# Second attention of a routed-experts kernel: four pieces of ScalarE's hand-written order placed in other half steps

## The reference, cut to what matters

```
xn  = layernorm(x, g_in)
q   = (xn @ Wq)  -> 16 heads of 64, scaled;   k, v = xn @ Wkv  (one k and v for all heads)
sim = q k^T + bias, with a null key in front, causal and padding masks
z   = layernorm(softmax(sim) v @ Wo, g_out)
scores = sigmoid(z @ router_w.T);  the best 4 of 8 groups, in them the best 8 of 64 experts
x   = x + sum over the 8 experts e of w_e * relu2(z @ up_e) @ down_e + shared expert
```

## Time and profile before

| | |
|---|---|
| median of three runs | 1869.3 us (1865.94 to 1871.79) |
| the profiled execution's own time | 1868.09 us |
| its span, first to last instruction | 1866.2 us |
| mean granted TensorE clock | 0.938 |
| busy over the span | TensorE 83%, its weight loads 65%, VectorE 64%, GpSimd 50%, ScalarE 44% |
| second attention, half steps 0 to 63 | about 690 to 1242 us of the span |
| the 19 rounds behind them | to about 1350 us |
| second expert layer | about 1356 us to the end |

### The profile page before, as it was taken

One profiled execution on the slowest core, in us unless ns is written; L12 is line 12 of the kernel. 1 busy time (PEld: TensorE's weight loads), 2 busy tenths in 40 slices (PEclk: granted clock), 3 DMA queues, 4 the chain that ended last, 5 costly groups with the idle time before them and its releaser, 6 DMA issues. The chain is left out here.

```text
span 1866.2 us, 35427 instructions
## 1 busy us (share of the span) xinstructions
PE 1542.3 (83%) x12186; PEld 1216.8 (65%) x12187; DVE 1187.6 (64%) x2849; ACT 826.3 (44%) x1614; POOL 940.9 (50%) x840
## 2 busy tenths in 40 slices
PE   5699999987888869999999999975058888888880
PEld 2588888864655547776777776654058877776770
DVE  2677677745777655578878778787024455666674
ACT  2233333323545334565565555643036564555550
POOL 1233333335665521115555555567627767776672
PEclk9899999989999989999999999997579999999995
DMA  5278458011000000001111111136666678998875
GB/s 152 61 192 219 117 152 235 1 32 51 25 13 24 12 24 1 1 2 52 61 58 55 61 61 58 55 117 244 181 210 189 191 221 265 285 278 259 268 210 158
DMA packets 151371, 226.33 MB, mean 121 GB/s; under 512 B 24779, under 2 KB 123730, under 8 KB 149079
## 3 DMA queue, kind: packets, MB, share of 16 engines
q1 hardware_dynamic: 109062, 115.11, 22.1%
q0 software_dynamic: 27648, 67.44, 10.2%
q10 hardware_dynamic: 14544, 42.21, 7.0%
HBM read 110.31 MB, written 122.75 MB: 125 GB/s over the span
## 5 line engine op out<-in xcount | busy, mean ns | idle before, releaser
L1927 POOL DMA_INDIRECT y_rows<-se_ys,se_yidx x320 | 325.2, 1016 | 162.8 <-issue 95.8
L1100 POOL DMA_INDIRECT x_slots<-wide,a_sidx x256 | 257.2, 1005 | 72.5 <-issue 72.5
L443 POOL TENSOR_TENSOR e_hl<-e_h,e_hh 128x512 fp32r<-128x512 f32 x80 | 103.5, 1294 | 227.7 <-ACT e_hh L427 227.7
L1089 POOL TENSOR_TENSOR flat<-flat,a_rs 128x512 f32<-128x512 f32 x64 | 69.8, 1091 | 269.7 <-DVE a_rs L1581 269.7
L1970 PE MATMUL ps<-wide,se_hT 128*128 x640 | 157.8, 390 | 31.2 <-DVE se_ys L2060 30.9
L1947 PE MATMUL ps<-ident,se_xs 128*128 128x128 f32 x640 | 89.1, 285 | 100.8 <-DMA se_xs<-x_slots 83.2
L1958 PE MATMUL ps<-se_xsT,se_up 128*128 128x128 f32 x1280 | 166.1, 285 | 5.3 <-DVE se_hT L2049 4.3
L1958 PEld LDWEIGHTS ps<-se_xsT,se_up 128*128 128x128 f32 x1280 | 155.8, 199 | 13.6 <-issue 9.9
L1947 PEld LDWEIGHTS ps<-ident,se_xs 128*128 128x128 f32 x640 | 74.9, 146 | 121.4 <-issue 84.6
L1970 PEld LDWEIGHTS ps<-wide,se_hT 128*128 128x128 f32 x640 | 117.2, 193 | 50.6 <-issue 37.5
L1991 ACT COPY se_up<-w_up 128x256 f32 x320 | 105.8, 402 | 99.5 <-issue 78.6
(11 more groups left out here) (283 smaller groups left out, 3613.8 us busy)
## 6 DMA issues: line engine op xcount, KB each, us to landing
x_slots<-wide SPq DMA_DIRECT2D x40, 1032.0 KB, 14.3
se_xs<-x_slots SPq DMA_DIRECT2D x80, 516.0 KB
se_got<-y_rows ACTq DMA_DIRECT2D x64, 512.0 KB, 4.8
w_up<-in_up SPq DMA_DIRECT2D x8, 1024.0 KB, 18.1
y_rows<-se_ys,se_yidx POOLq DMA_INDIRECT x320
wide<-in_xT SPq DMA_DIRECT2D x2, 2048.0 KB, 10.2
flat<-in_x SPq DMA_DIRECT2D x8, 512.0 KB, 3.9
x_slots<-wide,a_sidx POOLq DMA_INDIRECT x256, 2.9
```

The lines of the kernel that those rows point to most:

```text
L1100: pool.indirect_dma_start(out=x_slots, out_offset=bass.IndirectOffsetOnAxis(ap=sidx[:, r % 2, t, k_:k_ + 1], axis=0), in_=stage[:, t, k_, ...
L1927: pool.indirect_dma_start(out=y_rows, out_offset=bass.IndirectOffsetOnAxis(ap=yidx[:, w % 2, b:b + 1], axis=0), in_=ys[:, w % 2, b, :], in ...
```

## The change

Only the order of ScalarE's program in the second attention is different. `normalized` for half 0 of the next block is called at the end of half step 7 of the block before it, where it was called in half step 0 (in block 0 it stays there too, for block 1). `normalized` for half 1 moves from half step 5 to half step 3. `stage_z` of tiles 0, 1 and 2 moves from ages 6, 8 and 10 to ages 7, 9 and 11; tile 3 stays at age 12. No instruction is added or taken away, and the orders of TensorE, VectorE, GpSimd and the DMA queues are the same.

```diff
                     elif age == 6:
                         square(r, 2)
                         square(r, 3)
-                        stage_z(r, 0)
-                    elif age in (8, 10, 12):
-                        stage_z(r, age // 2 - 3)
+                    elif age in (7, 9, 11, 12):
+                        stage_z(r, (7, 9, 11, 12).index(age))
...
                     if i == 0:
                         queries(b, 1, 2)
                         keys_values(b, 1)
-                        normalized(b + 1, 0)
+                        if b == 0:
+                            normalized(1, 0)
...
                     if i == 3:
                         queries(b + 1, 0, 1)
+                        normalized(b + 1, 1)
                     elif i == 5:
                         queries(b + 1, 0, 2)
                         queries(b + 1, 0, 3)
                         keys_values(b + 1, 0)
-                        normalized(b + 1, 1)
...
                     elif i == 7:
                         queries(b + 1, 1, 0)
                         queries(b + 1, 1, 1)
+                        normalized(b + 2, 0)
```

## The result

The changed kernel took 1856.6 us, the median of six runs (1850.09 to 1859.83), beside 1867.8 us for the kernel before in six runs on the same chip (1865.94 to 1871.79). The medians lie 11.2 us apart. The ratio on record, 0.9928 with a 95% interval of 0.9911 to 0.9945, is not the quotient of these two medians (0.9940) and says 13.4 us less, 10.3 to 16.6. The kernel is faster, by more than the 8.8 us of the forecast.

The account below looks back on a forecast made before the run. TensorE was taken to bound the stage, busy 69.6 of 74 us per block. Terms 6.0 + 2.8 + 0 = 8.8 us off the profiled 1868.1 gave 1859.3, plus 1.2 for the median: 1860.5 us, range 1854.5 to 1867.0.

Parts of the forecast that it names:

- Half step 2, 5 x 1.2 us: Blocks 2 to 6: TensorE's wait for VectorE's read shrinks from 1.47 to 0.3 us, 6.0 us won in all.
- Block 7's nearly unchanged wait: Block 7, half step 2: 1.36 us wait, put down to TensorE arriving an estimated 0.9 us earlier.
- Half step 6, 6 x 0.46 us: Blocks 1 to 6: without the normalizing ScalarE is in time for L1240, saving 0.46 us each, 2.8 us.
- The stagings: Half steps 1 and 3: the stagings of tiles 1 and 2, 2.0 us each, cost nothing.
- The reserve behind it: Behind half step 1's staging: ScalarE may be 1.3 us later before further lateness returns as TensorE's wait.
- Block 0, 0 us: Projection comes 1.85 us later in half step 4, 1.85 us sooner in half step 6; they cancel, 0 us.
- The clock, "I take neither": Block 0: 1.7 us of lower granted clock may vanish, or appear at half step 4; counted as nothing.
- Rival 1: Staging in half step 1 eats half step 2's gain if table switches hold ScalarE twice: 1866.5 us; chance 0.18.
- Rival 2: All of the 1.47 and 0.71 us waits goes, plus 1.7 us of clock in block 0: 1855.9 us; chance 0.14.
- Rival 3: Clock falls more often where TensorE stands still, two per block in seven blocks: slower, 1884 us; chance 0.04.
- Rival 4: ScalarE is late in half steps 3 and 4 by as much as early elsewhere: 1869.3 us; chance 0.06.

Follow-up runs that it names:

- block 0's edit: The whole change, but in block 0 the normalizing of half 1 is called in half step 4 instead of 3: 1855.8 us, ratio 0.9941.
- the run with two stagings: The change, but tiles 0 and 1 are both staged at age 9, in half step 1: a single run of 1863.0 us.

## Why the prediction was right and where it was wrong

**Half step 2, 5 x 1.2 us: right.** The wait went from 1.47 to 0.28 in blocks 2 to 6, 1.19 us each. The lateness was ScalarE's, handed on by VectorE. That either move alone cures it shows it twice more. Block 7's nearly unchanged wait is one of another kind, as argued: ScalarE was not late there (0.58 us idle before its copy), and from the transposes of half step 1 to its wait TensorE has 8.6 us of work, where it has 9.5 in block 2.

**Half step 6, 6 x 0.46 us: right,** 0.71 to 0.25 us in six blocks, and half 1's normalizing alone does it.

**The stagings: right that they cost nothing, but they also bring nothing.** The prediction counted both pieces, 3.9 us, against a lateness of 1.2, and did not say that one of them was enough. Their cover in half step 1 was used up exactly (0.30 us of reserve).

**The reserve behind it: right in size.** It was put at 0.3 + 1.0 = 1.3 us. ScalarE 1.7 us later made a block 0.39 us longer.

**Block 0, 0 us: right in the waits** (1.90 us instead of the 2.1 foretold at half step 4, none at half step 6). The prediction left out a third wait of before, 0.91 us of TensorE for the normalizing in half step 6 (L1181), but the sum still comes out near nothing: from half step 4 on, block 0 takes 28.1 us with the change, and 28.3 in the two executions of before that have no fall there.

**The clock, "I take neither": this is the step that failed.** The prediction put the clock at nothing. It looked for falls in block 0 alone, since the one block that it had read by stretches, block 3, stood at 1.00. Blocks 1, 4 and 5 of that same execution had falls, which the same view would have shown. Against that first profile the term is worth 4.0 us: 12.7 us of stage less 8.7 of waits. On the means of three executions it is about 2: 10.8 less 8.7. Of these 2.1 us, 1.1 lie in block 0 (0.6 of it is the fall of the earlier trace rows, worth 1.7 us and present in one execution of three, 0.2 are waits, and 0.3 the clock at the stage's start), 0.5 in blocks 2 to 6, 0.6 in block 7, and block 1 takes back 0.1.

How much of this the change caused is shown only in part. The falls in blocks 2 to 6 came with the wait of half step 2, the very one that the change removes: 12 in 25 blocks with it, none in 45 without it. Those in block 0 came with its wait in half step 6: 2 in 5 profiles with it, none in 9 without it. These two hold about 1.1 us. Block 1 keeps its stand, and behind it the clock fell in every profile of the change and in two of three of before; block 7 had a fall in every profile of the change and in one of three of before, where there were two; what these blocks gave or took is not explained.

**The sum.** The forecast of 1860.5 us lies 3.9 us above the measured 1856.6, which is 0.4 us below the forecast's own range of 1857 to 1864. Of the 3.9, 1.5 us are the starting point: the median of three runs was 1869.3 us, that of six 1867.8. The other 2.4 us are near the 2.1 us that the stage won beyond the waits.

The two ratios say 13.4 and 13.7 us, with 10.3 and 9.4 as their lower ends, where the stage has 10.8 and the mean spans of three profiles each, 1863.9 and 1853.9 us, lie 10.0 apart. No further gain outside the stage is shown. The normalizing alone and the change with block 0's edit, with the same stage, came to 0.9931 and 0.9941 beside a larger set of runs of before. Over all fast executions on record, 50 of before and 13 of the change have means of 1867.5 and 1855.8 us, 11.7 apart with a 95% interval of 2.0 to either side. What a program takes outside the stage went from 1313.7 to 1320.6 us over the 14 profiles, so that a difference of 1 to 3 us can't be read there.

**The rivals.** Rival 1 falls by the run with two stagings and by the waits. Rival 2 named nearly the measured time (1855.9), in part by luck: no wait went to nothing, and the fall in block 0 that it wanted back was there in one execution of before out of three. Its direction, that more comes back than the waits, was right. Rival 3 was upside down: fewer stands, fewer falls. Rival 4 falls with the blocks' 72.5 us.

## What to carry to other kernels

An engine that runs at 44% can still be the cause of the bound engine's waits: follow a wait back along an unbroken chain to the first instruction that began late, and ask by how much. Whatever removes that much is enough, and a second piece moved for the same reason brings nothing.

Where TensorE's granted clock falls behind a wait, as it did here behind about half of the waits of 1.46 us, the wait costs more than its own length. Read the clock by stretches over all repetitions of the pattern, not in one of them, and in more than one execution: one profile of this kernel was 3 us off another in the same stage.

## What the runs showed of the hardware that was not expected

- Stands of 1.46 to 1.59 us, in blocks where TensorE is busy for 69.6 of 74 us, were followed by a fall of the granted clock (0.57 over the 4 us of the lines shown) in 12 of 25 cases and not in the others; with 0.27 us at the same place there was none in 45. Such a fall cost 0.2 to 0.4 us of a block, as far as the other waits took it up: a block of 74.15 us took 74.38 and 74.56 us.
- The same stand of 2.46 us in block 1 was followed by no fall in 2 of 14 profiles, by one that cost 1.7 us in 7 and by one that cost 3.1 us in 5.
- A table load of 1.28 us held ScalarE for its own length and no longer: the next instruction began 0.01 us behind it for the square root and 0.02 us for the exponential.
